# Attention inside a two-branch block: Q and K projected once per batch and placed by DMA, values with ones as weight tile, packed reciprocals, row maxima in pieces of 256

## What is computed

```python
# x: (2, 1024, 128); 16 heads; q has 8 lanes a head, k and v have 64
q = (x @ Wq + bq).reshape(B, T, 16, 8)
k = (x @ Wk + bk).reshape(B, T, 16, 64)
v = (x @ Wv + bv).reshape(B, T, 16, 64)
qc = einsum('bthd,dl->bthl', q, Wc)            # Wc: (8, 64)
att = einsum('bthl,bshl->bhts', qc, k) / 8      # causal mask, softmax over s
y = einsum('bhts,bshl->bthl', softmax(att), v).reshape(B, T, 1024)
x = x + y @ Wo + bo
```

## Time and profile before

| | |
|---|---|
| median of 3 runs | 1095.69 us (1095.19 to 1096.35) |
| the profiled execution | 1095.54 us, span 1093.8 us |
| TensorE busy | 930.0 us (85%) |
| VectorE, ScalarE, GpSimd busy | 547.0, 356.9, 367.3 us |
| chain that ended last | PE 73%, DVE 8%, POOL 8%, issue 5%, DMA 3% |
| mean granted TensorE clock | 0.943 |

### The profile page before, as it was taken

One profiled execution on the slowest core, in us unless ns is written; L12 is line 12 of the kernel. 1 busy time (PEld: TensorE's weight loads), 2 busy tenths in 40 slices (PEclk: granted clock), 3 DMA queues, 4 the chain that ended last, 5 costly groups with the idle time before them and its releaser, 6 DMA issues.

```text
span 1093.8 us, 17199 instructions
## 1 busy us (share of the span) xinstructions
PE 930.0 (85%) x5887; PEld 750.1 (69%) x5887; DVE 547.0 (50%) x1503; ACT 356.9 (33%) x701; POOL 367.3 (34%) x550
## 2 busy tenths in 40 slices
PE   2338699990988999999999999999999847799993
PEld 1225477770347889797988498897899834577773
DVE  6753254544375746455463656382721373345554
ACT  2101133330224353443431543434354211232323
POOL 2677256562003111111110011444321037266661
PEclk9999799996699999999999999999999958799996
DMA  9510355544000000000000000101000000455535
GB/s 357 199 47 24 105 171 159 182 130 157 20 0 21 1 21 1 20 1 1 20 1 1 0 21 1 40 22 38 16 9 1 22 23 20 125 161 171 183 105 196
DMA packets 79285, 76.31 MB, mean 70 GB/s; under 512 B 10409, under 2 KB 69947, under 8 KB 78454
## 3 DMA queue, kind: packets, MB, share of 16 engines
q1 hardware_dynamic: 70006, 63.15, 18.6%
q0 software_dynamic: 9216, 12.33, 3.4%
HBM read 48.13 MB, written 30.21 MB: 72 GB/s over the span
## 4 chain that ended last, share of the span: by engine, by line
PE 73%; DVE 8%; POOL 8%; issue 5%; DMA 3%; ACT 1%; SPq 1%; POOLq 0%; DVEq 0%; ACTq 0%
PE PS L1238 24%; PE PS L1149 8%; PE PS L1218 7%; POOL xbuf L452 7%; PE PS L1200 6%; PE PS L1136 6%; PE PS L1137 5%; PE PS L1180 3%; PE PS L1289 3%; PE PS L1157 2%; PE PS L1110 2%; PE PS L1203 1%; PE PS L1182 1%; PE PS L1273 1%; DVE xs L900 1%
## 5 line engine op out<-in xcount | busy, mean ns | idle before, releaser
L1238 PE MATMUL PS<-area_v,pT 128*128 128x128 f32 x2304 | 316.3, 277 | 2.9 <-POOL pT L464 2.9
L1238 PEld LDWEIGHTS PS<-area_v,pT 128*128 128x128 f32 x2304 | 305.4, 192 | 13.3 <-POOL pT L464 3.0
L606 ACT ACTIVATE pT<-PS 128x512 f32<-128x512 f32 (+3 forms) x384 | 185.5, 491 | 248.2 <-PE PS L1218 245.7
L464 POOL TENSOR_SCALAR_AFFINE_SELECT pT<-pT 128x128 f32<-128x128 f32 x256 | 79.1, 313 | 467.0 <-ACT pT L606 466.6
L918 DVE TENSOR_REDUCE mxp<-PS 128x2 f32<-128x1024 f32 (+2 forms) x192 | 180.8, 955 | 83.1 <-PE PS L1203 69.5
L483 POOL DMA_INDIRECT ybuf<-area_o,yidx x160 | 155.7, 973 | 126.5 <-DVE area_o L877 87.5
L452 POOL DMA_INDIRECT xbuf<-xn,sidx x128 | 125.3, 979 | 110.4 <-issue 63.7
L1218 PE MATMUL PS<-Qc,Kz 128*128 128x512 f32 (+3 forms) x384 | 156.4, 411 | 6.3 <-ACT pT L606 3.7
L1200 PE MATMUL PS<-Kz,Qn 128*128 128x512 f32 (+3 forms) x384 | 117.9, 389 | 4.0 <-DVE mxp L918 3.3
L561 ACT ACTIVATE area_o<-PS 128x320 f32<-128x320 f32 x128 | 56.0, 437 | 145.1 <-PE PS L1137 136.2
L869 DVE TENSOR_TENSOR area_o<-area_o,PS 128x320 f32<-128x320 f32 x128 | 62.5, 488 | 78.2 <-ACT area_o L561 75.1
(11 more groups left out here) (172 smaller groups left out, 930.1 us busy)
## 6 DMA issues: line engine op xcount, KB each, us to landing
area_v<-xbuf SPq DMA_DIRECT2D x32, 340.0 KB, 3.2
area_v<-in_L_ffn_wg_dram SPq DMA_DIRECT2D x32, 256.0 KB, 3.3
area_v<-in_L_ffn_wu_dram SPq DMA_DIRECT2D x32, 256.0 KB, 3.6
area_v<-in_L_ffn_wd_dram SPq DMA_DIRECT2D x64, 128.0 KB, 2.5
yg<-ybuf SPq DMA_DIRECT2D x24, 256.0 KB, 4.3
xbuf<-Kz SPq DMA_DIRECT2D x4, 1360.0 KB, 10.4
ybuf<-Kz SPq DMA_DIRECT2D x2, 2048.0 KB, 10.3
Kz<-Kn SPq DMA_DIRECT2D x32, 128.0 KB, 2.4
```

Of the source, the lines that this page charges most:

```text
L464: nc.gpsimd.affine_select(out=block_, in_=block_, pattern=[[1, P]], compare_op=ALU.is_ge, fill=zero, base=0, channel_multiplier=-1).then_i ...
L606: nc.scalar.activation(pT[:, N % 4, 0:w], PS[:, 4 + N % 2, 0:w], ACT.Exp).then_inc(exp_done, 1)
L1238: ins = mm(PS[:, 6 + half, (i % 4) * P:(i % 4 + 1) * P], pT[:, N % 4, k * P:(k + 1) * P], area_v[:, (j * NH + h) * VW:(j * NH + h) * VW + ...
```

## The change

- Q and K of a whole batch are projected by four matmuls (`project`), biases are added on evacuation, the high and low parts go to a DRAM buffer `qkbuf` by three DMAs each (`projected`), and each group's 26 rows per head come back with eight DMAs (`group_in`) into `Qx` and `Kz`. Batch 1's projections stand in group 3.
- A step covers 256 queries (128 in the first two of a unit) by 128 keys of two heads; a group has 40 steps in four units of 4, 8, 12 and 16 steps. Each step has two matmuls for the scores, one exp, and PV with `value_and_ones` as the weight tile, so that the output has values on 64 partitions and the sum, repeated, on 64.
- Row work (scores for maxima in pieces of up to 256 by two heads, maxima turned, and the other inserted work) is one list, `ROW_ITEMS`, with about one item in every step, in two PSUM banks used in turn. An item may start when the item two before it is done.
- Per unit, ScalarE copies sums of four heads into one tile (`sums`) and the values unnormalised into `yT` (`latents`); VectorE inverts the packed sums in two halves (`invert`); SP spreads them with eight DMAs (`spread_sums`); GpSimd multiplies (`scale`). The output stage has no transposes.
- The combination in group 0 is cut into four parts. `fold` is shorter.

Cut to its core:

```diff
+TC = 256
+NCH = T // TC
+STEPS = [(c, j, p) for c in range(NCH) for j in range(2 * c + 1, -1, -1) for p in range(2)]
+SLOT = len(STEPS)
 LAG = 3
+DIAG = [n for n, (c, j, p) in enumerate(STEPS) if j >= 2 * c]
+UNIT_END = [max(n for n, (c, j, p) in enumerate(STEPS) if c == u) for u in range(NCH)]
...
+def row_items(Gi):
+
+    late = 3
+    items = []
+    for c in range(NCH):
+        pieces = [("R", i, k, min(TC, (i + 1) * P - k * TC), hp, (i, k, hp) == (2 * c + 1, c, 1))
+                  for i in (2 * c, 2 * c + 1) for k in range(c + 1) for hp in range(2)]
+        if c:
+            pieces.insert(late, ("T", Gi, c - 1))
+        elif Gi:
+            pieces.insert(late, ("T", Gi - 1, NCH - 1))
+        items += pieces
+    if Gi == 0:
+        items = [("J", 0, q, h) for q in range(2) for h in range(2)] + items
+    if Gi == G_LN1 + 1:
+        items[8:8] = [("X", 0), ("X", 1)]
+    if Gi == NG - 1:
+        items[20:20] = [("J", 1, q, h) for q in range(2) for h in range(2)]
+    if Gi == NG + 1:
+        items.insert(2, ("C",))
...
+LEAD = 6
+ROW_STEP = [SLOT * (Gi - 1) + LEAD + k * SLOT // len(row_items(Gi)) for Gi in range(B * NG) for k in range(len(row_items(Gi)))]
...
+EVAC, RECIP, SCALE_AT, DRAIN = LAG + 1, LAG + 5, LAG + 10, 16
...
 # SP
+            def group_in(Gi):
+
+                b, g = Gi // NG, Gi % NG
+                for j in range(2):
+                    sp.wait_ge(qk_out[j], 16 * 6 * (b + 1))
+                if Gi >= 2:
+                    sp.wait_ge(st_ready, SLOT * (Gi - 1))
+                for hh in range(HG):
+                    rows = slice(RW * hh, RW * hh + RQ)
+                    sp.dma_start(Qx[Gi % 2][rows, :].bitcast(F32), qkbuf[b, 0, HG * g + hh]).then_inc(qk_in[Gi % 2], 16)
+                    sp.dma_start(Kz[Gi % 2][rows, hh, :].bitcast(F32), qkbuf[b, 1, HG * g + hh]).then_inc(qk_in[Gi % 2], 16)
+
+            def spread_sums(U):
+
+                sp.wait_ge(rec_ready, U + 1)
+                if U >= 2:
+                    sp.wait_ge(norm_done, U - 1)
+                for hh in range(HG):
+                    for a in range(2):
+                        first = LAT * (hh % 2) + RW * a
+                        sp.dma_start(rden[U % 2][first:first + RW, hh // 2, :], den[U % 2][RW * hh:RW * hh + RW, :])\
+                            .then_inc(rep_done[U % 2], 16)
...
 # GpSimd, in each step
+                    for U in units_at(N, SCALE_AT, Gi // NG):
+                        scale(U)
+                    if n in DIAG:
                         pool.wait_ge(exp_done, N + 1)
+                        w = step_width(n)
+                        for a in range(2):
+                            block_ = pT[:, N % 4, a * w:a * w + P]
+                            ins = nc.gpsimd.affine_select(out=block_, in_=block_, pattern=[[1, P]], compare_op=ALU.is_ge,
+                                                          fill=zero, base=0, channel_multiplier=-1)
+                        ins.then_inc(mask_done, 1)
...
+            def scale(U):
+
+                Gi, c = U // NCH, U % NCH
+                pool.wait_ge(y_free, 2 * (U + 1))
+                pool.wait_ge(rep_done[U % 2], 16 * 2 * HG * (U // 2 + 1))
+                y = yT[:, 2 * (Gi % NG):2 * (Gi % NG) + 2, c * TC:(c + 1) * TC]
+                nc.gpsimd.tensor_tensor(y, y, rden[U % 2][:], ALU.mult).then_inc(norm_done, 1)
...
 # ScalarE
+            def high_part(k):
+
+                _, b, q, half = ROW_ITEMS[k][1]
+                n = 4 * b + 2 * q + half
+                act.wait_ge(row_ps, k + 1)
+                if n >= 2:
+                    act.wait_ge(qk_out[n % 2], 16 * 3 * (n // 2))
+                nc.scalar.activation(stage[n % 2][0][:], PS[:, k % 2, :], ACT.Identity, bias=qkb[:, q:q + 1]).then_inc(high_ready, 1)
+
+            def sums(U, p):
+
+                act.wait_ge(pv_done, UNIT_STEP[U] + 1)
+                if U >= 2:
+                    act.wait_ge(rep_done[U % 2], 16 * 2 * HG * (U // 2))
+                for a in range(2):
+                    hh = 2 * p + a
+                    ins = nc.scalar.activation(den[U % 2][RW * hh:RW * hh + RW, :],
+                                               PS[LAT * (1 - a):LAT * (1 - a) + RW, pv_bank(U, a), TC * p:TC * p + TC], ACT.Copy)
+                ins.then_inc(den_ready, 1)
...
 # VectorE
+            def row_max(Gi, k):
+                _, i, c, w, hp, last = ROW_ITEMS[k][1]
+                dve.wait_ge(row_ps, k + 1)
+                nc.vector.tensor_reduce(mxp[:, i, c, 2 * hp:2 * hp + 2], PS[:, k % 2, 0:2 * w].rearrange("p (h w) -> p h w", h=2),
+                                        AX.X, ALU.max).then_inc(row_done, 1)
+                if last:
+                    dve.wait_ge(row_done, k + 1)
+                    max_parts(i // 2)
...
+            def invert(U, half):
+
+                dve.wait_ge(den_ready, 2 * U + 2)
+                part = den[U % 2][:, P * half:P * half + P]
+                ins = nc.vector.reciprocal(part, part)
+                if half:
+                    ins.then_inc(rec_ready, 1)
...
                 for n in range(SLOT):
+                    N = SLOT * Gi + n
+                    for k in rows_at(N):
+                        row_item(k)
+                    inverses(N, Gi // NG)
+                    if Gi == G_COMB and n in (2, 4, 6, 8):
+                        combine_part(0, 1, 2 * (n // 2 - 1), 2)
...
 # TensorE
+            def row_item(k):
+
+                Gi, item = ROW_ITEMS[k]
+                if k >= 2:
+                    pe.wait_ge(row_done, k - 1)
...
+            def row_scores(k, Gi, i, c, w, hp, last):
+
+                pe.wait_ge(qk_in[Gi % 2], 16 * 2 * HG * (Gi // 2 + 1))
+                diag = c == i // 2
                 for hh in range(2):
+                    ins = mm(PS[:, k % 2, hh * w:(hh + 1) * w], Qx[Gi % 2][:, i * P:(i + 1) * P],
+                             Kz[Gi % 2][:, 2 * hp + hh, TC * c:TC * c + w], start=(hh == 0), stop=not diag, skip_group_check=True)
+                if diag:
+                    ins = mm(PS[:, k % 2, 0:2 * w].rearrange("p (h w) -> p h w", h=2)[:, :, w - P:w], identb[:],
+                             causS[:].unsqueeze(1).broadcast_to([P, 2, P]), start=False, stop=True, skip_group_check=True)
+                ins.then_inc(row_ps, 1)
...
             def s_cols(Gi, n):
...
+                for a in range(2):
+                    ins = mm(PS[:, 2 + N % 2, a * w:(a + 1) * w], Kz[Gi % 2][:, 2 * p + a, j * P:(j + 1) * P],
+                             Qx[Gi % 2][:, t1 - w:t1], start=(a == 0), stop=True, skip_group_check=True)
+                ins.then_inc(st_ready, 1)
...
             def pv(Gi, n):
...
+                if n in DIAG:
+                    pe.wait_ge(mask_done, len(DIAG) * Gi + DIAG.index(n) + 1)
                 else:
                     pe.wait_ge(exp_done, N + 1)
+                for a in range(2):
+                    h = (Gi % NG) * HG + 2 * p + a
+                    ins = mm(PS[:, pv_bank(U, a), (p + 1) * TC - w:(p + 1) * TC], value_and_ones(j, h), pT[:, N % 4, a * w:(a + 1) * w],
+                             start=(first and p == 0), stop=(j == 0), skip_group_check=True)
                 ins.then_inc(pv_done, 1)
```

More of the change, by code:

```diff
@@ L61 @@
 R0 = 2
-VW = LAT + 1
+RQ = R0 + 3 * HD
+VP = 3 * LAT
 SCALE = 1.0 / 8.0
@@ new lines, with rows_at @@
+LEAD = 6
+ROW_ITEMS = [(Gi, item) for Gi in range(B * NG) for item in row_items(Gi)]
+ROW_STEP = [SLOT * (Gi - 1) + LEAD + k * SLOT // len(row_items(Gi)) for Gi in range(B * NG) for k in range(len(row_items(Gi)))]
+ROW_NUMBER = {item if item[0] != "R" else (Gi, item): k for k, (Gi, item) in enumerate(ROW_ITEMS)}
+def rows_at(step):
+    return [k for k, s in enumerate(ROW_STEP) if s == step]
+EARLY = [k for k, s in enumerate(ROW_STEP) if s < 0]
+EVAC, RECIP, SCALE_AT, DRAIN = LAG + 1, LAG + 5, LAG + 10, 16
@@ L93, with units_at @@
+UNIT_STEP = [SLOT * Gi + UNIT_END[u] for Gi in range(B * NG) for u in range(NCH)]
+def units_at(step, delay, b):
+    return [U for U, s in enumerate(UNIT_STEP) if s + delay == step and U // (NCH * NG) == b]
 LAST = [(0, 1), (1, 3), (3, 6), (6, 8)]
@@ new lines, in _, with projected @@
+            sp.wait_ge(s_ax, 1)
+            for b in range(B):
+                sp.dma_start(qkbuf[b, 0, :, 0:R0, :], Kz[0][0:2 * NH, 1, :].bitcast(F32)).then_inc(qk_const, 16)
+                sp.dma_start(qkbuf[b, 1, :, 0:R0, :],
+                             rden[0][0:4 * NH].rearrange("p a t -> p (a t)")).then_inc(qk_const, 16)
+            def projected(k):
+                _, b, q, half = ROW_ITEMS[k][1]
+                n = 4 * b + 2 * q + half
+                cols = slice(512 * half, 512 * half + 512)
+                high, low = stage[n % 2]
+                sp.wait_ge(row_done, k + 1)
+                for r, part in enumerate((high, high, low) if q == 0 else (high, low, high)):
+                    sp.dma_start(qkbuf[b, q, :, R0 + HD * r:R0 + HD * r + HD, cols], part[:].bitcast(F32))\
```

(41 more changed lines are left out.)

499 lines of the change are left out of this document (207 added, 292 removed).

## The result

| | before | changed |
|---|---|---|
| median | 1096.02 us (4 runs) | 1078.26 us (4 runs, 1074.56 to 1083.32) |
| ratio | | 0.984, interval 0.981 to 0.987 |
| span of the profiled execution | 1093.8 us | 1076.7 us |

A forecast was written before the change was run, and what follows sets the result against it. TensorE was taken to bound the head groups, busy 60.1 of 60.6 us in a middle one. On 1095.5 us, -41.4 + 3.6 + 27.8 - 15.6 + 2 + 19.1 + 18.7 = +14.2 gave 1109.7, say 1110 us; range 1076 to 1130.

The forecast's parts named there:

- mask waits: Head groups: TensorE waits 1.7 us in eleven places for causal masks queued behind GpSimd's multiplication, +18.7 us (0 to 28).
- single waits: Places where VectorE, ScalarE or routing newly stops TensorE, from group 0 to batch 1's start: +19.1 us (5 to 28).
- More, shorter matmuls: Head groups: 32 more column and 32 more row score matmuls a group, 0.058 us each, +27.8 us; masks and PV zero.
- Batch 1's start: Start of batch 1's heads: routing ends after heads could start, with none of today's cover left, +5 us.
- the layer norm: Group 1: 5.6 us on VectorE, and ScalarE waits for its statistics before the next exp, +3.2 us.
- the slots: Batch 1, from 631.06 to 635.6: 4.5 us as one block, costing +2.5 us.
- batch 1's projections: ScalarE's third projection waits for DMAs queued on SP, with that step's exp queued behind it, +5 us.
- The combination: Group 0's first nine steps: combining expert results on VectorE stops TensorE 6 us, net +3.4 after today's mask stop.
- The spread sums: Rival, chance 0.30: the inverted sums reach GpSimd's multiplication in time, 0.2 us lost per place, 1093 us or down to 1079.
- two banks: Rival, chance 0.15: each of 316 row items costs TensorE 0.1 us waiting for VectorE, 32 us more, 1140 us.
- weight loads: Rival, chance 0.07: 128 fewer PV weight loads a group at 0.05 us each give 51 us back, 1060 us.
- the first rival: The rival that the spread sums are in time, chance 0.30; its lower bound set the range's low end.

The follow-up runs named there:

- c_scale17: The changed kernel with GpSimd's multiplication 17 steps after a unit's end instead of 13: 1054.12 us, 0.962 of the kernel before.

## Why the prediction had the wrong sign

| step of the sum | forecast | the runs |
|---|---|---|
| projections out of seven groups | -41.4 | about -46: their 28 products 1.1 us each and not 0.95; the bias matmuls were not tried alone |
| 480 score matmuls more | +27.8 | about +7 (0.015 each, by difference) |
| PV's passes, fewer and wider | 0 | -8 |
| causal matmuls, fewer and wider | 0 | -5.3 |
| output stages | -15.6 | -13.6 |
| prologue | +2 | +3.7 |
| mask waits | +18.7 | 20.2 in the trace, 25 when removed |
| single waits | +19.1 | about 10 |
| work at half clock | no term | about +3.5 |

**The step that failed** is the work term of "More, shorter matmuls": "each has 0.058 us on top", and in the next lines "nothing" for the masks and "I cost this at zero" for PV. The 0.058 came from a pair of matmuls behind PV, 0.33 us less its columns, divided by two. But a pair of 512 in that place has the same 0.11 us on top as a pair of 256, and four of 256 in place of two of 512 have 0.13: most of it is paid once where the kind of work changes, and one more matmul of 256 columns adds 0.01 to 0.03. The two zeros err the other way: merging passes gives something back. The rows of 128 and 512 columns show the same time per column to about 2%, and 8 us are 2.5% of PV's 316 us of busy time before: the rows could not exclude it.

A middle group shows the size. The forecast's terms give 60.1 - 5.9 + 3.7 = 57.9 us of work; at full clock and without waits it is 52.7, so 5.2 less. Of these PV is 0.9, the causal matmuls 0.9, and the products of the projections 0.6 (four at 1.1 and not 0.95). That takes 2.8 of the 3.7 off the 64 score matmuls: they cost about 0.9 us, 0.015 each. This last number is a difference and not a run of its own; the step of 1.33 us, with 0.05 on top of everything, agrees with it.

Over all groups the prices make 20.6 (scores) + 8 + 5.3 + 4.2 (products) = 38 us less than forecast. Half clock takes 3.5 back, and the last seven row pieces of group 0, which stood in the prologue, are now in its first six steps, 1.7 us by their columns. That makes 33 where 29.4 were measured; 3.5 us stay open.

A smaller reading: the blocks of a projection are put 1.48 us apart, while the lines of the earlier trace rows show 1.38 between the first two; later ones of the same kernel are 1.48 apart (452.88 to 454.36), so it changes 0.1 us a group.

**Mask waits** were right in place, cause and size: 19.2 us in the eleven places named (18.7 forecast), 20.2 us in all. The multiplication on GpSimd, costed without a row of its own, took 1.27 us, just above the upper bound of 1.2. Removing them gives 25 us; 1.4 of the 5 us between are the half clock behind one of them, and the changed kernel's own runs are 9 us apart, so the rest is not explained.

**Single waits.** Batch 1's start 4.9 us (forecast 5), the layer norm 2.5 (3.2), the slots 2.0 (2.5), batch 1's projections 1.5 on the staging buffer and about 2.5 on exp (5) came as described. The combination is where it was too high: 2.5 us of waits for VectorE and not 6. The stop at batch 1's start also holds most of the half clock, which the forecast left out. The forecast took the kernel before's own waits off only at the combination; the added idle time of 30 us less the 20.2 of the masks leaves about 10 of 19.1.

**The rivals.** The spread sums were not in time, two banks do not pace everything (TensorE is busy for 52.7 of 52.7 us in a middle group of `c_scale17`), and weight loads were not binding in the sense of 51 us; but fewer and wider PV passes do pay, and 8 us of that rival were real. The result came from none of them: it is the forecast's own mechanism with a smaller work term. That the range of 1076 to 1130 holds the result is no merit of the sum: its low end was the first rival's.

## What to carry to other kernels

A pair of matmuls timed behind another kind of work overstates what one more matmul costs. Time pairs of two widths: what does not change with the width is paid per pair. Then price a cut by the width that comes out of it: here a piece whose columns still take 0.107 us cost 0.01 to 0.03, and one whose columns take 0.053 cost 0.04 to 0.1. Price merges by the same list, with the opposite sign. Take prices from groups at full clock without waits, since in whole executions waits and half clock move with the change. And when an engine runs in program order, put a wait for a long DMA chain behind the short work that another engine needs: here two numbers in one line moved the result from 0.984 to 0.962.
